# Four chained attention layers: layer 2's attention regrouped into 32-row and 32-column groups of the matrix engine

## The reference

```python
q = hidden_state @ Wq + bq                    # 32 heads x 8
k = encoder_hidden_state @ Wk + bk            # 8 heads x 8
v = encoder_hidden_state @ Wv + bv            # 8 heads x 8
scores = jnp.einsum('bkgld,bksd->bkgls', q, k) * scale + encoder_attention_mask[:, :, None, :, :]
attn = jax.nn.softmax(scores, axis=-1)
out = jnp.einsum('bkgls,bksd->bkgld', attn, v)
x = out @ Wo + bo + hidden_state              # then a layer norm
```

## Time and profile before

| what | value |
|---|---|
| median of 3 runs | 1823.73 us (1823.61 to 1826.17) |
| the profiled execution | 1823.94 us, of it the span of the trace 1822.2 us |
| busy share of the span: PE, DVE, ACT, POOL | 91%, 53%, 43%, 23% |
| layer 2's attention stage | from 1262.8 to 1480.7 us of the span |
| in that stage, each 25 us in the middle (two pairs): PE, DVE, ACT, POOL busy | 25.00, 22.40, 18.10, 17.89 us |

### The profile page before, as it was taken

The page is one execution under the profiler, slowest core; times in us unless marked ns, Lnnn a source line. Parts: engine busy times, 40 slices in busy tenths (PEclk is TensorE's granted clock), DMA queues, the critical chain, the costliest instruction groups (busy, mean ns, idle before and its releaser), DMA issues. The chain is left out here.

```text
span 1822.2 us, 34031 instructions
## 1 busy us (share of the span) xinstructions
PE 1665.0 (91%) x13322; PEld 1397.0 (77%) x13322; DVE 964.8 (53%) x2086; ACT 783.5 (43%) x1544; POOL 425.1 (23%) x483
## 2 busy tenths in 40 slices
PE   4978999999999889999999998697999958999598
PEld 3656888888888758888888887587677746887497
DVE  6873534344353544343534444753889865554643
ACT  4644343534344344344343533422677732333421
POOL 2012020110200120201102000700777764221600
PEclk9989999999999989999999999799999978999699
DMA  3021010000100120100001000202100001000001
GB/s 97 0 70 35 1 47 1 24 24 1 35 1 1 44 61 1 47 1 24 24 1 36 1 1 1 67 0 39 34 0 0 0 7 51 2 3 2 1 1 46
DMA packets 48453, 38.09 MB, mean 21 GB/s; under 512 B 10626, under 2 KB 45384, under 8 KB 48200
## 3 DMA queue, kind: packets, MB, share of 16 engines
q1 hardware_dynamic: 48328, 36.30, 6.8%
HBM read 34.20 MB, written 2.10 MB: 20 GB/s over the span
## 5 line engine op out<-in xcount | busy, mean ns | idle before, releaser
L939 DVE TENSOR_REDUCE att_rmax<-psum 128x6 f32<-128x390 f32 (+1 forms) x96 | 49.2, 512 | 400.8 <-PE psum L771 400.8
L914 ACT ACTIVATE att_q_sb<-psum,split_cols 128x512 f32<-128x512 f32 x128 | 88.4, 690 | 295.3 <-PE psum L807 294.6
L852 PE MATMUL psum<-att_wo_hi,att_ot_hi 128*128 128x256 f32 x512 | 149.4, 292 | 2.8 <-DVE att_ot_lo L968 2.8
L852 PE MATMUL psum<-att_wo_lo,att_ot_hi 128*128 128x256 f32 x512 | 144.8, 283 | 0.0
L852 PE MATMUL psum<-att_wo_hi,att_ot_lo 128*128 128x256 f32 x512 | 144.8, 283 | 0.0
L835 PE MATMUL psum<-att_pt,att_v_sb 128*128 128x128 f32 x1024 | 122.2, 278 | 1.0 <-ACT att_pt L923 1.0
L835 PEld LDWEIGHTS psum<-att_pt,att_v_sb 128*128 128x128 f32 x1024 | 116.8, 192 | 3.3 <-issue 1.5
L917 ACT ACTIVATE att_k_sb<-psum,split_cols 128x512 f32<-128x512 f32 x128 | 88.5, 691 | 70.9 <-PE psum L807 70.9
L807 PE MATMUL psum<-split_feat_hi,att_wqk_hi 128*128 128x512 f32 x256 | 105.3, 411 | 12.8 <-DVE att_pt L933 12.8
L977 DVE TENSOR_TENSOR g_x_res<-psum,g_x_res 128x256 f32<-128x256 f32 x128 | 54.3, 424 | 110.5 <-PE psum L852 77.7
L721 POOL CAST att_wqk_hi<-w_stage_qk 128x512 fp32r<-128x512 f32 x28 | 17.1, 610 | 401.3 <-PE psum L807 396.7
(11 more groups left out here) (292 smaller groups left out, 4287.7 us busy)
## 6 DMA issues: line engine op xcount, KB each, us to landing
ln_wo<-in_L_xattn_wo SPq DMA_DIRECT2D x2, 2048.0 KB
w_stage_qk<-in_L_xattn_wq SPq DMA_DIRECT2D x32, 128.0 KB, 2.3
w_stage_qk<-in_L_xattn_wk SPq DMA_DIRECT2D x32, 128.0 KB, 2.7
w_stage_vo<-in_L_xattn_wv SPq DMA_DIRECT2D x8, 512.0 KB, 4.0
w_stage_vo<-in_L_xattn_wo SPq DMA_DIRECT2D x8, 512.0 KB, 4.0
c_ctx_tok<-in_ctx SPq DMA_DIRECT2D x4, 512.0 KB, 5.4
g_x_res<-in_x SPq DMA_DIRECT2D x4, 512.0 KB, 8.7
m_w<-in_L_xattn_w_fc SPq DMA_DIRECT2D x2, 1024.0 KB, 6.2
```

The costliest lines, as they stand in the source:

```text
L852: mm = pe.matmul(o_ps[p % 2], a, b, start=(h == 0 and t == 0), stop=(not last and h == HG - 1 and t == 2))
L914: act.activation(q_sb[:, h, :], q_ps[:, :], ACT.Identity, bias=G.cols[:, i - 1, head:head + 1]).then_inc(q_ready, 1)
L939: dve.tensor_reduce(rmax[:, a:b], s_ps[group][:, :, :], X_AXIS, ALU.max).then_inc(max_done, 1)
```

## The change

The stage is replaced by a new one, `phase_grouped_attention`. The scores' shape (2048 columns per pair) and the sequence of the softmax stay. What differs:

- **Scores.** The array is used as four groups of 32 rows. Each group holds four key/value heads of 8 features, so `k_bd` has 4 blocks instead of 8 (DVE places 512 columns per pair instead of 1024). A pair has 8 matmuls of 32 rows and 256 moving columns, each group writing a bank of its own, instead of 4 of 128 rows and 512 columns.
- **Context.** 16 matmuls with 32 stationary columns, four column groups, instead of 16 with 64. One ACT instruction of 256 columns moves it, instead of eight of 64.
- **Softmax.** It goes in two halves of 1024 columns per pair instead of four units of 512. Only the normalising multiplication stays at 512 columns, and writes its result permuted.
- **Values.** They take the context tokens as stationary operand directly, so the two copies into `vx` per pair go.
- **Bias.** The output bias and the value bias are folded into one row before the loop and added by a third matmul in `outputs`; POOL's addition per pair goes. Before the loop there are two more matmuls, and PE's first projection waits for the folded bias (`bias_done`).
- **Order.** Everything is written out, without a hardware loop. In each round t PE does scores(t-1), projections(t), context(t-3), half of the transposes(t-2), outputs(t-3), the other half.

The core of the diff; the removed function is printed above:

```diff
-def phase_narrow_attention(nc, A, G, layer, w, dst, loads=()):
...
+def phase_grouped_attention(nc, A, G, w, dst, loads=()):
...
+        q_sb, k_bd = m.sb("q_sb", [P, 2, 2, 2, T]), m.sb("k_bd", [P, 2, 4, P])
+        v_bd = m.sb("v_bd", [P, 4, 2, 2, 2 * ROWS])
+        soft = m.sb("soft", [P, 2, TILES, 4, 2, T])
+        prob = m.sb("prob", [P, TILES, 2, 4, T])
+        pt = m.sb("pt", [P, 2, TILES, 2, 2, P])
...
+        s_ps, t_ps = m.ps("s_ps", (P, TILES, 4, 2, T)), m.ps("t_ps", (P, 2, 2, 2, P))
+        p_bank, c_bank = m.ps("p_bank"), m.ps("c_bank")
+        q_ps, k_ps, v_ps = p_bank[:, 0:D].rearrange("p (c n) -> p c n", c=2), p_bank[:, D:D + P], p_bank[:, D + P:D + P + 64]
+        c_ps, o_ps = c_bank[:, 0:D].rearrange("p (b c t) -> p b c t", b=2, c=2), c_bank[:, 0:D]
...
+                def subtract(p, half):
+                    pool.wait_ge(max_done, 2 * p + half + 1)
+                    s = wide(soft, p, half).rearrange("p i v b t -> p (i v b) t")
+                    pool.tensor_tensor(s, s, rmax[:, half, :].unsqueeze(2).to_broadcast([P, 16, T]), ALU.subtract).then_inc(shifted, 1)
+                def normalize(p, half):
+                    pool.wait_ge(inv_done, 2 * p + half + 1)
+                    if p:
+                        pool.wait_ge(t_psum, 2 * p + half - 1)
+                    for n in range(2):
+                        i = 2 * half + n
+                        pool.tensor_tensor(prob[:, i, :, :, :].rearrange("p b v t -> p v b t"), soft[:, p % 2, i, :, :, :],
+                                           rinv[:, half, 8 * n:8 * n + 8].rearrange("p (v b) -> p v b", v=4).unsqueeze(3)
+                                           .to_broadcast([P, 4, 2, T]), ALU.mult).then_inc(prob_ready, 1)
...
+                for t in range(PAIRS + 2):
+                    if there(t - 2):
+                        normalize(t - 2, 0)
+                    if there(t - 1):
+                        subtract(t - 1, 0)
+                    if there(t - 2):
+                        normalize(t - 2, 1)
+                    if there(t - 1):
+                        subtract(t - 1, 1)
...
+                def project(p):
+                    x_new, ctx = (t[:, :, p * P:(p + 1) * P] for t in (G.feat_f, G.ctx_f))
+                    if p:
+                        pe.wait_ge(k_done, p)
+                    for c in range(2):
+                        accumulate(q_ps[:, c, :], [(wq[:, k, c * P:(c + 1) * P], x_new[:, k, :]) for k in range(KT)])
+                    accumulate(k_ps, [(wk[:, k, :], ctx[:, k, :]) for k in range(KT)])
+                    accumulate(v_ps, [(ctx[:, k, :], w.wkv[:, k, 1, :]) for k in range(KT)]).then_inc(p_psum, 1)
+                def scores(p):
+                    pe.wait_ge(q_done, p + 1)
+                    pe.wait_ge(k_done, p + 1)
+                    if p:
+                        pe.wait_ge(masked, 2 * p)
+                    for b in range(2):
+                        for i in range(TILES):
+                            rows = slice(ROWS * i, ROWS * (i + 1))
+                            mm = pe.matmul(s_ps[:, i, :, b, :], q_sb[rows, p % 2, b, :, :].rearrange("p c t -> p (c t)"),
+                                           k_bd[rows, p % 2, :, b * T:(b + 1) * T], start=True, stop=True)
+                    mm.then_inc(s_psum, 1)
+                def turn(p, half):
+                    pe.wait_ge(prob_ready, 4 * p + 2 * half + 2)
+                    if p or half:
+                        pe.wait_ge(pt_done, 2 * p + half)
+                    for n in range(2):
+                        for b in range(2):
+                            for q in range(2):
+                                mm = pe.transpose(t_ps[:, n, b, q, :],
+                                                  prob[:, 2 * half + n, b, 2 * q:2 * q + 2, :].rearrange("p v t -> p (v t)"), G.ident[:, :])
+                    mm.then_inc(t_psum, 1)
+                def context(p):
+                    pe.wait_ge(pt_done, 2 * p + 2)
+                    pe.wait_ge(v_done, p + 1)
+                    if p:
+                        pe.wait_ge(x_done, p)
+                    for b in range(2):
+                        for q in range(2):
+                            for i in range(TILES):
+                                mm = pe.matmul(c_ps[ROWS * i:ROWS * (i + 1), b, :, :].rearrange("p c t -> p (c t)"),
+                                               v_bd[:, p % 4, b, i % 2, ROWS * q:ROWS * (q + 1)], pt[:, p % 2, i, b, q, :],
+                                               start=(q == 0), stop=(q == 1))
+                    mm.then_inc(c_psum, 1)
+                def outputs(p):
+                    pe.wait_ge(ot_done, p + 1)
+                    for c in range(2):
+                        pe.matmul(o_ps, ot[:, c, :], w.wo[:, c, :], start=(c == 0), stop=False)
+                    pe.matmul(o_ps, one[:, :], w.o_bias[0:1, :], start=False, stop=True).then_inc(o_psum, 1)
...
+                pe.wait_ge(bv_done, 1)
+                accumulate(bias_ps, [(bv_wide[:, :], w.wo[:, c, :]) for c in range(2)]).then_inc(bias_psum, 1)
+                pe.wait_ge(w_ready, 1)
+                pe.wait_ge(bias_done, 1)
+                pe.wait_ge(one_made, 1)
+                for t in range(PAIRS + 3):
+                    if there(t - 1):
+                        scores(t - 1)
+                    if there(t):
+                        project(t)
+                    if there(t - 3):
+                        context(t - 3)
+                    if there(t - 2):
+                        turn(t - 2, 0)
+                    if there(t - 3):
+                        outputs(t - 3)
+                    if there(t - 2):
+                        turn(t - 2, 1)
...
+                def move_projected(p):
+                    act.wait_ge(p_psum, p + 1)
+                    if p >= 2:
+                        act.wait_ge(s_psum, p - 1)
+                    if p >= 4:
+                        act.wait_ge(c_psum, p - 3)
+                    for c in range(2):
+                        a = act.activation(q_sb[:, p % 2, :, c, :], q_ps[:, c, :].rearrange("p (b t) -> p b t", b=2),
+                                           ACT.Identity, bias=cols[:, c:c + 1])
+                    a.then_inc(q_done, 1)
+                    for b in range(2):
+                        for u in range(2):
+                            a = act.activation(
+                                v_bd[T * u:T * u + T, p % 4, b, :, :].rearrange("p h (q x) -> p h q x", x=16)[:, :, 0:4:3, 8 * u:8 * u + 8],
+                                v_ps[T * b:T * b + T, :].rearrange("p (h q u d) -> p h q u d", h=2, q=2, u=2)[:, :, :, u, :], ACT.Copy)
+                    a.then_inc(v_done, 1)
+                def move_context(p):
+                    act.wait_ge(c_psum, p + 1)
+                    if p:
+                        act.wait_ge(o_psum, p)
+                    act.activation(ot[:, :, :].rearrange("p c (b t) -> p b c t", b=2), c_ps, ACT.Copy).then_inc(ot_done, 1)
...
+                for t in range(PAIRS + 3):
+                    if there(t - 2):
+                        exponent(t - 2, 1)
+                    if there(t):
+                        move_projected(t)
+                    if there(t - 3):
+                        move_context(t - 3)
+                    if there(t - 2):
+                        move_turned(t - 2, 0)
+                    if there(t - 1):
+                        exponent(t - 1, 0)
+                    if there(t - 2):
+                        move_turned(t - 2, 1)
...
+                def add_mask(p, half):
+                    if half == 0:
+                        dve.wait_ge(s_psum, p + 1)
+                    if p >= 2:
+                        dve.wait_ge(prob_ready, 4 * (p - 2) + 2 * half + 2)
+                    dve.scalar_tensor_tensor(wide(soft, p, half).rearrange("p i v b t -> p (i v) (b t)"),
+                                             s_ps[:, tiles(half), :, :, :].rearrange("p i v b t -> p (i v) (b t)"), score_scale,
+                                             mask[:, 2 * p:2 * p + 2, :].rearrange("p b t -> p (b t)").unsqueeze(1)
+                                             .to_broadcast([P, 8, P]), ALU.mult, ALU.add).then_inc(masked, 1)
+                    dve.wait_ge(masked, 2 * p + half + 1)
+                    if p:
+                        dve.wait_ge(shifted, 2 * p + half - 1)
+                    dve.tensor_reduce(rmax[:, half, :], wide(soft, p, half).rearrange("p i v b t -> p (i v b) t"),
+                                      X_AXIS, ALU.max).then_inc(max_done, 1)
+                def invert(p, half):
+                    dve.wait_ge(exp_done, 2 * p + half + 1)
+                    dve.tensor_reduce(rsum[:, half, :], wide(soft, p, half).rearrange("p i v b t -> p (i v b) t"),
+                                      X_AXIS, ALU.add).then_inc(sum_done, 1)
+                    dve.wait_ge(sum_done, 2 * p + half + 1)
+                    if p:
```

(30 more changed lines are left out.)

382 lines of the change are left out of this document (71 added, 311 removed).

## The result

| what | before | after |
|---|---|---|
| median (range, runs) | 1824.95 us (1823.61 to 1826.21, 4) | 1773.6 us (1771.2 to 1776.97, 4) |
| ratio after / before | | 0.972, 95% interval 0.9699 to 0.9741 |
| profiled execution, its span | 1823.94, 1822.2 us | 1776.97, 1775.3 us |
| layer 2's stage, to its last addition | 217.8 us | 167.3 us |

The kernel is 51 us faster, and 1770.0 us (1761 to 1788) was forecast. The profiled span is 46.9 shorter: 50.5 less in the stage, 2.1 more ahead of it and 1.5 more behind it, where nothing was changed.

The account below looks back on a forecast made before the run. PE was taken as the bound before, the ring after. Stage end 1278.9 + 7.0 + 14 x 8.83 (123.6) + 17.3 = 1426.8 instead of 1480.66, 53.9 less than the profiled 1823.94: 1770.0 us, range 1761 to 1788.

Parts of the forecast that it names:

- ring: One round's chain through POOL, PE and DVE: subtraction, normalising, transposes, scores, mask, maximum; 8.83 us per pair.
- stage start to the end of the first maximum: Stage's fill: first projection waits for the folded bias, scores at half clock; first maximum at 1278.9.
- round 1: First pair's maximum to the second's: masks and maxima, keys, first sum and reciprocal; 7.0 us.
- round 2: Second pair's maximum to the third's: the first of 14 rings of 8.83 us, 123.6 together.
- from the last first-half maximum to the end: Stage's end, where nothing overlaps: subtraction, exponential, normalising, transposes, context, output, last addition; 17.3 us.
- rival 5: DVE's own work is the bound: 8.4 to 8.6 us per pair, 1763 to 1767; chance 0.55 together with the forecast.
- rivals 1 and 3: Rival 1: small costs add up, 1776 to 1786, chance 0.18; rival 3: groups run one after another, 1815, chance 0.06.
- rival 2: POOL becomes the bound through dearer subtraction and permuted write: 10.0 us per pair, 1786; chance 0.12.
- full granted clock after the fill: Sign expected in the changed profile: PE at full clock after the stage's fill; 0.5 in the middle would refute the prediction.
- Rival 4: PE idles about 1.5 us per round and its clock halves: 14.3 us per pair, 1853; chance 0.04.
- PE bounds the kernel now: Stage before: PE, busy 25.00 of 25 us, comes first at 12.5 us per pair, DVE close behind.
- short waits: Rest of PE's pair in the kernel before, beyond its summed work of 11.7 of 12.5 us.

Follow-up runs that it names:

- the ring was shortened: Kernel after with second transposes behind the next scores, 1780.77 us; with keys placed by ACT, 1783.81 us; with both edits, 1772.46 us.
- the two experiments: Kernel after with each score matmul issued four times, 1822.09 us; kernel after with each context matmul issued four times, 1799.6 us.
- filler: Kernel after plus unread identity transposes on PE ahead of some waits, 1771.59 us; with second transposes behind scores and second exponential ahead of its move too, 1767.89 us.

## Why the prediction was right, point by point

The sign, the size and the mechanism of the new pace held; what the prediction said of the bound before did not (last point). 1770.0 was 3.6 below the median, and 7.0 below the profiled run. The terms, in us:

| term | forecast | measured |
|---|---|---|
| ring per pair | 8.83 | 8.76 |
| stage start to the end of the first maximum | 16.1 | 15.7 |
| round 1, to that of the second pair | 7.0 | 8.49 |
| round 2 | 8.83 | 10.57 |
| the other 13 rounds | 114.8 | 114.3 |
| from the last first-half maximum to the end | 17.3 | 18.3 |

- **The ring.** Its parts, which add up to 8.85 and not to the 8.83 written, were right within 0.1: the subtraction 1.904 (1.92 forecast, from the factor of the earlier trace rows), normalising with its handover 2.10 (2.19), transposes with handover 1.02 (0.96), scores and handover 1.22 (1.17), mask 1.26 (1.31). Its lead over DVE alone was slim, 0.28, so rival 5 (DVE's own work is the bound) was close, and when the ring was shortened the exponential's place in ACT's queue came next. The prediction named DVE as next, and not this.
- **The groups overlap.** The scores' 16 records take 1.15 and the context's 32 records 1.08. The records added by the two experiments cost 2.59/48 = 0.054 and 2.62/96 = 0.027 each, where 0.053 and a lower bound of 0.028 were taken (rivals 1 and 3 were wrong). As to the drain at a change of tiling mode that the Trainium skill gives (TensorEngine Tiling (Array Packing), Key Properties): eight transposes take 1.02 up to the start of the scores, which change the mode, and 0.93 up to that of the output's matmuls, which don't (1335.04 to 1335.97). So this change costs about 0.1 here, and not a whole tail of 0.28; 0.1 was taken.
- **Two slips changed nothing.** POOL's 2 x 1.92 + 4 x 1.0 is 7.8 and not 7.9, and the chances add up to 0.99.
- **DVE, POOL.** 24.08 of 25 busy, and 8.48 instead of 8.4 per pair; POOL did not become the bound (rival 2).
- **Projections hide.** So they do directly behind the scores and behind the context. Ahead of the scores they don't; that this was their price was not in the prediction.
- **The clock: the term that was mis-sized.** The prediction had "full granted clock after the fill", and in the fill half clock only for the bias and the first scores. Round 2 is 1.7 over its forecast: the transposes and scores of the third pair ran at the lower level, which is the whole 1.8 us by which it exceeds the pace. Round 1 is 1.5 over, and here a second term was missing. The projections behind the first scores ran at the lower level, ACT moved them late, and only then loaded its table for the exponential, 1.28 us. DVE waited 1.53 for that exponential. With filler the projections were through earlier, table load and first subtraction ended together near 1279.8, and the round took 7.61; the prediction had no term for that load. The drain is 1.0 over: its subtraction ended on time (5.8 us behind the maximum, 6.0 forecast), but the exponential stood in ACT's queue behind the move of eight transposes that took 1.97 at the lower level. One round in the middle took 9.24, 0.5 more than the pace. Against these stand 0.4 less up to the first maximum and about 1 less in the other rounds, since the ring was 0.07 shorter than forecast: in all the stage is 3.3 longer than its sum. The remaining 3.6 of the profiled run's 7.0 lie outside the stage (2.1 ahead of it, 1.5 behind). Rival 4 had the right mechanism (idle time, then the lower level) and the wrong extent: it comes in stretches, not for good. That idle time has to do with the level is supported by filling it: the stretches in the middle went.
- **"PE bounds the kernel now"** was the weakest step, and it failed. Of 1.9 us of PE's work per pair, 0.27 came back; the prediction's own sum for PE, 11.7 of 12.5, had left 0.8 as "short waits". The forecast did not fall with it, since it was summed from the new ring and not from PE's saving. Had the change only made PE's matmuls cheaper and left the units at 512 columns, a forecast by PE's sum would probably have been far off; that kernel wasn't run.

## What to carry to other kernels

Forecast from the ring that one round passes through, with each part start to start, and name the second limit before counting a saving: an engine that is busy for 25 of 25 us can be worth only 0.3 us per pair, and small waits on its weight loads are a sign of that. When a ring is shortened, look at what stands ahead of the critical instruction in each queue it passes, also in the first round, where ACT's table load stands. Look at PE's idle time too, since the granted clock can take back what the order gains. If PE waits in every round, a few matmuls that nobody reads may be worth more than the next reordering.

## What the runs showed of the hardware

- With PE idle in each round its clock fell in some rounds and not in others: after the same 1.23 us, scores at 1.15 and at 1.85. With six more transposes in the gap there was no fall in 100 us.
- Four column groups of 32 run side by side like row groups: 128 records in 3.70 us, and 0.027 for each that was added, where a record with 64 stationary columns took 0.116 in the kernel before. No row of before showed this shape.
- POOL's subtraction of 1024 columns with a broadcast second operand took 1.904, less than the 2.409 of the form without. The two also differ in output type, and no run tells which of the two it is.
- ACT's table load ahead of the first exponential took 1.28 us. In the kernel before it stood at 1269.21, where ACT had nothing to do; in the kernel after it stood at 1282.90, ahead of work that was due.
- Placing the keys takes 1.50 us on ACT in four instructions of 128 columns and 0.74 on DVE in one of 512.
